# Two stages of a six-stage decoder share one block of programs: the routed experts' closing norm and the first input products of a state space layer

## The chip, the core and the metric

The kernel runs on one core of a Trainium2 chip, in one launch. The metric is the device time of that core in microseconds. In the order in which this text names them, the engines are TensorE (PE, matrix products and transposes), VectorE (DVE), ScalarE (ACT), GpSimd (POOL) and SyncE (SP, which issues most transfers). Each runs its own program in order and meets the others only through semaphores.

## The reference

Six stages run over 2048 tokens of width 256, in fp32. Each ends with the sum with its input and a norm over the 256 features. Stages 3 and 4 are those that the change touches.

```python
x = _layernorm(x + _L0_attn_ref(x, ...))              # stage 1: attention
x = _layernorm(x + _L0_xattn_ref(x, ctx, ctx, gamma)) # stage 2
x = _layernorm(x + _L0_ffn_ref(x, ...))               # stage 3: top 2 of 8 experts + a shared one
x = _layernorm(x + _L1_attn_ref(x, ...))              # stage 4: state space layer
x = _layernorm(x + _L1_xattn_ref(x, ctx, mask, ...))  # stage 5
x = _layernorm(x + _L1_ffn_ref(x, ...))               # stage 6: experts with LoRA

# stage 4, with u = x
zxbcdt = u @ W_in.T
z, xBC, dt = jnp.split(zxbcdt, [D_INNER, D_INNER + CONV_DIM], axis=-1)
for k in range(D_CONV):                               # 4 taps along the tokens
    conv = conv + xp[:, k:k + l, :] * conv_w[:, k]
xBC = silu(conv)
dt = softplus(dt + dt_bias)
y = _chunked_scan(xh, dt, -exp(A_log), Bh, Ch, D)     # decays exp(segsum(dt*A))
y = group_norm(y * silu(z)) * norm_weight
return y @ W_out.T
```

## The kernel before

The 2048 tokens are 16 tiles of 128 tokens (on the 128 partitions), and 4 chunks of 4 tiles. `resid` holds the tokens between stages as tiles, `residT` the same values turned, with the features on the partitions, as the next stage's products need them. One Python function for each stage opens one `nc.Block` with a hand written program for each of the five engines; the order inside an engine is the order of the code. The block's end is an event of every engine, in which POOL also drains its queue, and before each new function `recycle` (L86 to L95) has a barrier over all engines, a clearing of all semaphores on POOL, and a second barrier. Nothing of one block therefore overlaps the next.

**Stage 3** (`layer0_experts`, L1196, block L1267, names with `c_`) first routes, then runs 39 slots of 128 gathered token rows through the expert weights (SP loads slot s's rows into `c_xrow`, in 4 buffers; POOL sends each slot's output away with an indirect transfer), then adds up by halves of a chunk: SP brings the rows back, DVE combines them and takes mean and variance (`combine`, L1400 to L1413), POOL makes scale and shift by `variance_power` (L1305 to L1311, the last of it `c_shift`). Behind that come tile by tile: ACT's `apply` (L1337, writes `resid`), PE's `turn_back` (L1575, two transposes into a bank `cps_x`), ACT's `turned_out` (L1342, copies the bank to `residT`, one tile behind `apply`). In this text that part, 609 to 630 us, is the turning stretch.

**Stage 4** (`layer1_state_space`, L1620, block L1705, names with `d_`) starts with the time steps: eight products of `d_wdt` (L2082), four transposes (L2087), then DVE's softplus chain of 17 steps (`d_x` L1950 to `d_dt` L1973). The input product is dealt as jobs; in PE's program a job is a `fill` of a bank `dps_ip` (L2011; two products of 128 x 512, or for `mixed` four transposes, L2017), on ACT `evacuate` (for a job that is convolved, L1804 into `d_pad` and L1805 into `d_acc`; L1798 for the gate z), on DVE `convolve` (L1888, three instructions a job), on ACT `activate` (L1813). `own` are the eleven jobs of chunk 0 in their order: 0 to 5 the six that are convolved, 6, 7 and the next two of the gate, `mixed` at place 8. The scan goes by tiles q: PE's `segments` (L2030), ACT's `decay` (L1819), PE's `products` (L2042), DVE's `time` and `weigh`. After `products(0)` a loop over 23 slots runs to the stage's end at 827 us.

The constants of stage 4 are loaded at the head of SP's program: `d_wdt`, `d_bias`, `d_alog` for the time steps, `d_win` (768 KB) with two small ones for the convolution, then `d_wz` and the rest with `d_wout`.

Of the kernel before, what the change touches and what calls it, by code (L numbers as in the profile page):

```python
# [25 lines left out]
P = 128  # L26
# [35 lines left out]
class Kernel:  # L62
# [26 lines left out]

    def recycle(self):  # L90
# [1092 lines left out]
def experts_weights(k, ctx):  # L1183

    k.ahead, k.ahead_in = [], k.sem("c_weights_in")
    w = {}
    for name, shape, dt in (("wr", [P, KD, 32], F32), ("descending", [P, NE], F32), ("tables", [P, 256], F32),
                            ("lower", [P, P], BF16), ("wsg", [P, KD, SHARED], F32), ("wsu", [P, KD, SHARED], F32),
                            ("wsd", [P, 3, D], F32), ("wgu", [P, KD, NE, 2 * EF], F32), ("wd2", [EF // 2, NE, 2, D], F32)):
# [3 lines left out]
    return w  # L1193


def layer0_experts(k, w):  # L1196

# [9 lines left out]
    routed = nc.dram_tensor("routed", (2 * NTOK + XSLOTS * P, D), F32, kind="Internal").ap()  # L1207
    with ExitStack() as ctx:
# [10 lines left out]

        lg, best, cand = sb("lg", [P, TILES, E]), sb("best", [P, TILES, E]), sb("cand", [P, TILES, E])  # L1220
        masks, maxima = many(2, "mask", [P, TILES, E]), many(2, "max", [P, TILES])
        top, ex, total = sb("top", [P, TILES]), sb("ex", [P, TILES, E]), sb("total", [P, TILES])
        gate = many(2, "gate", [P, TILES])
# [4 lines left out]
        xr = sb("xr", [P, TILES, ROW])  # L1228
        acc = sb("acc", [P, TILES, D])
# [4 lines left out]
        back = [many(2, f"back{n}", [P, TPC, D]) for n in range(2)]  # L1234
# [7 lines left out]
        ltT = sb("ltT", [P, CHUNK])  # L1242
# [20 lines left out]

        def live(s):
            return 0 <= s < XSLOTS

        with nc.Block() as block:  # L1267
            @block.sync
            def _(sp):
                for n in range(2):  # L1270
                    sp.wait_ge(scattered[n], 16 * TILES)
                for s in range(XSLOTS):
                    if s >= 4:
                        sp.wait_ge(x_turned, s - 3)
                        sp.wait_ge(target_done, s - 3)
                    sp.dma_start(xrow[s % 4][:], k.xrows[s * P:(s + 1) * P, :]).then_inc(x_in[s % 4], 16)
                for v in range(4):
                    sp.wait_ge(sent[v], 16 * len(range(v, XSLOTS, 4)))
                for h in range(2 * NCHUNK):
                    c, half = divmod(h, 2)  # L1280
                    if h >= 2:
                        sp.wait_ge(back_in[h % 2], 32 * (h // 2))
                    if h >= 4:
                        sp.wait_ge(r_done, 2 * (h - 3))
                    for n in range(2):
                        first = n * NTOK + h * 2 * P
                        sp.dma_start(back[n][c % 2][:, 2 * half:2 * half + 2, :], routed[first:first + 2 * P, :].rearrange("(t p) f -> p t f", p=P)
                                     ).then_inc(back_in[h % 2], 16)

            @block.gpsimd  # L1290
            def _(gp):
                def scatter(t, n):
                    gp.indirect_dma_start(k.xrows[:], bass.IndirectOffsetOnAxis(ap=place_int[n][:, t:t + 1], axis=0),  # L1293
                                          xr[:, t, :], None).then_inc(scattered[n], 16)

                def send(s):
                    gp.wait_ge(out_done, s + 1)
                    gp.wait_ge(target_done, s + 1)
                    gp.indirect_dma_start(routed[:], bass.IndirectOffsetOnAxis(ap=target[s % 8][:], axis=0),  # L1299
                                          out[s % 4][:], None).then_inc(sent[s % 4], 16)  # L1300

                def variance_power(c):
                    u = c % 2
                    gp.wait_ge(mv_done, TPC * (c + 1))
                    gp.tensor_scalar(rstd[u][:], mv[u][:, :, 1], EPS, None, ALU.add).then_inc(eps_done, 1)  # L1305
                    gp.wait_ge(eps_done, c + 1)
                    gp.tensor_tensor(rstd[u][:], rstd[u][:], k.mhalf[:, 0:TPC], ALU.pow).then_inc(rstd_done, 1)
                    gp.wait_ge(rstd_done, c + 1)
                    gp.tensor_tensor(shift[u][:], mv[u][:, :, 0], rstd[u][:], ALU.mult).then_inc(product_done, 1)
                    gp.wait_ge(product_done, c + 1)  # L1310
                    gp.tensor_scalar(shift[u][:], shift[u][:], -1.0, None, ALU.mult).then_inc(shift_done, 1)  # L1311

                gp.wait_ge(placed, 2)
                gp.wait_ge(rows_copied, TILES + 2)
# [303 lines left out]


def layer1_state_space(k):  # L1620

# [1445 lines left out]
```

## Time and profile before

| | us |
|---|---|
| median of 3 runs | 1281.39 |
| the runs | 1274.37, 1281.39, 1285.85 |
| profiled execution, its own time | 1271.11 |
| span of the profile | 1269.0 |
| stage 3, closing part (shared expert, combine, turning stretch) | 592 to 630 |
| last work of stage 3 to first product of stage 4 | 630.3 to 637.8 |
| stage 4 | 637.8 to 827.8 |

The time lies 2.1 us over the span, which is what comes before the first and after the last recorded instruction. The profiled execution is 10.3 us shorter than the median and inside the range of the runs. TensorE's clock has two levels, and a granted clock of 1.00 or 0.50 means the upper or the lower, and a figure between a mixture within the stretch.

### The profile page before, as it was taken

What the parts mean: (1) busy time and instruction counts of PE and PEld (TensorE: products, weight loads), DVE (VectorE), ACT (ScalarE), POOL (GpSimd) and SP (SyncE); (2) the same over time, 40 slices, a digit from 0 to 9 for tenths busy, and PEclk for the clock granted to TensorE, in tenths of its full rate; (3) what the DMA queues carried; (4) which work ended last, traced back from release to release, by engine and by line L of the source; (5) the groups of instructions that cost most, each with busy time, mean ns of one, the idle gap of its engine ahead of it and who ended that gap; (6) DMA issues with size and microseconds to landing.
All of it is one profiled execution on the core that took longest, in us unless ns stands there. A gap on an engine that the chain in (4) does not pass through costs nothing. (4 is left out here: it accounts for less than half of the span.)

```text
span 1269.0 us, 20972 instructions
## 1 busy us (share of the span) xinstructions
PE 1112.9 (88%) x7484; PEld 662.5 (52%) x7484; DVE 781.2 (62%) x1531; ACT 575.9 (45%) x1199; POOL 455.1 (36%) x692
## 2 busy tenths in 40 slices
PE   6888779988888588999579998789998899999997
PEld 3566544454443245776234455567786343545455
DVE  4889887888884322333667677736566355555554
ACT  2666516766677301333455664256664322122120
POOL 6999852545542263333224445421111000000001
PEclk7999969999999799999789999989999899999999
DMA  6658244655652023333323000000000000000000
GB/s 217 202 174 275 81 124 122 150 137 148 146 130 53 25 84 96 105 109 101 99 65 141 1 1 1 1 1 2 2 2 1 25 1 0 9 9 9 8 9 25
DMA packets 73115, 91.72 MB, mean 72 GB/s; under 512 B 12691, under 2 KB 61997, under 8 KB 72333
## 3 DMA queue, kind: packets, MB, share of 16 engines
q1 hardware_dynamic: 68595, 80.72, 22.6%
q0 software_dynamic: 3408, 9.34, 2.1%
q8 instruction: 62, 1.02, 0.4%
q10 hardware_dynamic: 1010, 0.31, 0.1%
q14 instruction: 40, 0.33, 0.1%
HBM read 55.37 MB, written 29.17 MB: 67 GB/s over the span
## 5 line engine op out<-in xcount | busy, mean ns | idle before, releaser
L919 ACT ACTIVATE a_late<-a_qkv 128x512 f32<-128x512 f32 x128 | 77.2, 603 | 58.9 <-PE a_qkv L996 58.9
L2546 POOL TENSOR_SCALAR f_rstd<-f_mv 128x1 f32<-128x1 f32 x16 | 3.8, 240 | 267.9 <-DVE f_mv L2685 267.8
L867 DVE TENSOR_REDUCE b_nm<-a_s 128x4 f32<-128x1024 f32 x64 | 78.0, 1219 | 29.9 <-PE a_s L965 29.8
L2630 DVE TENSOR_TENSOR f_prod<-f_sg,f_kept 128x512 f32<-128x512 f32 (+1 forms) x48 | 33.2, 692 | 97.9 <-ACT f_kept L2575 95.0
L2755 PE MATMUL fps_h<-residT,w_f_w 128*128 128x512 f32 x176 | 83.9, 617 | 2.4 <-DVE f_inner L2667 2.4
L867 DVE TENSOR_REDUCE b_nm<-a_pt 128x4 f32<-128x1024 f32 x64 | 76.7, 1198 | 1.5 <-PE a_pt L965 1.5
L919 ACT ACTIVATE a_late<-a_y 128x512 f32<-128x512 f32 x128 | 76.9, 600 | 0.0
L2569 ACT ACTIVATE f_sg<-fps_h 128x512 f32<-128x512 f32 (+1 forms) x24 | 14.3, 596 | 126.6 <-PE fps_h L2774 109.8
L1011 PE MATMUL a_o<-a_late,b_vt 128*32 128x256 f32 x1024 | 69.2, 389 | 0.0
L1299 POOL DMA_INDIRECT routed<-c_out,c_target x39 | 37.5, 962 | 67.4 <-ACT c_out L1371 67.1
L1888 DVE SCALAR_TENSOR_TENSOR d_acc<-d_pad,d_cw,d_acc 128x512 f32<-128x512 f32 x72 | 57.8, 810 | 1.7
L351 POOL TENSOR_TENSOR a_nrm<-a_ss,phalf 128x20 f32<-128x20 f32 x16 | 57.0, 3560 | 4.2 <-DVE a_ss L473 4.2
L2755 PEld LDWEIGHTS fps_h<-residT,w_f_w 128*128 128x128 f32 x176 | 33.8, 196 | 42.9 <-issue 38.5
L1547 PE MATMUL cps_h<-c_wgu,c_xT 128*128 x156 | 52.7, 461 | 0.7 <-ACT c_xT L1359 0.6
L1486 DVE TENSOR_TENSOR c_hid<-c_sg,cps_h 128x176 f32<-128x176 f32 x39 | 13.2, 338 | 63.2 <-issue 50.6
L839 POOL TENSOR_TENSOR a_rest<-a_rest 128x256 f32<-128x256 f32 x16 | 11.6, 725 | 96.8 <-DVE a_rest L892 96.8
L1737 POOL TENSOR_TENSOR d_rs<-d_ms,mhalf 128x4 f32<-128x4 f32 x16 | 22.4, 1401 | 65.6 <-DVE d_ms L1945 65.6
L2011 PE MATMUL dps_ip<-residT,d_win 128*128 128x512 f32 x96 | 44.6, 598 | 0.3 <-ACT d_zs L1798 0.2
L1293 POOL DMA_INDIRECT xrows<-c_xr,c_place_int x32 | 31.1, 971 | 34.6 <-DVE c_xr L1456 19.3
L2569 ACT ACTIVATE f_sg<-f_kept 128x512 f32<-128x512 f32 (+1 forms) x24 | 15.1, 630 | 60.1 <-DVE f_kept L2635 60.1
L1566 PE MATMUL cps_o<-c_wd,c_hT 88*128 x156 | 40.1, 380 | 0.0
L1011 PEld LDWEIGHTS a_o<-a_late,b_vt 128*32 128x32 f32 x1024 | 26.9, 110 | 25.1 <-issue 14.0
(425 smaller groups left out, 2895.8 us busy)
## 6 DMA issues: line engine op xcount, KB each, us to landing
kparts<-a_rest SPq DMA_DIRECT2D x48, 192.0 KB, 3.2
a_rest<-a_rest SPq DMA_DIRECT2D x64, 128.0 KB, 3.1
xrows<-in_c_fill SPq DMA_DIRECT2D x13, 387.0 KB, 4.4
c_xrow<-xrows SPq DMA_DIRECT2D x39, 129.0 KB
c_back<-routed SPq DMA_DIRECT2D x16, 256.0 KB, 3.3
a_front<-kparts SPq DMA_DIRECT2D x12, 288.0 KB
a_front<-qparts SPq DMA_DIRECT2D x36, 96.0 KB
qparts<-b_xp SPq DMA_DIRECT2D x48, 64.0 KB, 2.8
```

The lines of the kernel that those rows point to most:

```text
L351: gp.tensor_tensor(nrm[v][:], ss[v][:], k.phalf[:, 0:H20], ALU.pow).then_inc(rooted, 1)
L867: dve.tensor_reduce(nm[s % 2][:, 4 * n:4 * n + 4].rearrange("p (g h) -> p g h", h=2), s1[step % 2][:], AX.X, ALU.max, negate=True).then_in ...
L919: act.activation(pr[g % 8][:], s2[g % 2][:], ACT.Exp, scale=SCALE).then_inc(s2_out, 1)
L1011: ins = pe.matmul(o_ps[32 * j:32 * j + 32, q % 2, :], vt[x % 2][:, lh, g, :], pr[g % 8][:, lh, :], start=(lh == 0), stop=(lh == KD - 1))
L1293: gp.indirect_dma_start(k.xrows[:], bass.IndirectOffsetOnAxis(ap=place_int[n][:, t:t + 1], axis=0), xr[:, t, :], None).then_inc(scattered[ ...
L1299: gp.indirect_dma_start(routed[:], bass.IndirectOffsetOnAxis(ap=target[s % 8][:], axis=0), out[s % 4][:], None).then_inc(sent[s % 4], 16)
L1547: ins = pe.matmul(h_ps[s % 2][:, 0:2 * F], xT[s % 2][:, kd, :], wgu[:, kd, ds(e, 1), :].rearrange("p a f -> p (a f)"), start=(kd == 0), st ...
L1566: ins = pe.matmul(o_ps[:, s % 2, 0:D], hT[s % 2][:, c, :], wd2[:, ds(e, 1), c, :].rearrange("p a f -> p (a f)"), start=(c == 0), stop=(c = ...
L1888: ins = dve.scalar_tensor_tensor(out=acc[v][:], in0=pad[v][:, :, tap:tap + T], scalar=cw[:, m, tap:tap + 1], in1=acc[v][:], op0=ALU.mult, ...
L2011: ins = pe.matmul(bank[:], win[:, kd, m * P:(m + 1) * P] if m < XT else wz[:, kd, (m - XT) * P:(m - XT + 1) * P], k.residT[:, kd, c * CHUN ...
L2630: dve.tensor_tensor(prod[n % 2][at], sg[n % 2][at], up, ALU.mult).then_inc(prod_done, 1)
L2755: pe.matmul(h_ps[j][:], (w1, w3)[j][:, kd, m * P:(m + 1) * P], k.residT[:, kd, c * CHUNK:(c + 1) * CHUNK], start=(kd == 0), stop=False)
```

## The change

The five programs of stage 3 become plain functions `sync`, `gpsimd`, `scalar`, `vector`, `tensor` that stage 4's block calls at the head of its own programs. Four of them take a hook `between` that stage 4 fills. The barrier pair and the clearing between all stages are gone (`recycle` is empty); the semaphores of the stages before are cleared on POOL at the start of stage 3 and at the start of stage 5 (`release`), without a barrier of their own beside the block's. Stage 4 takes over stage 3's PSUM banks: `cps_h` for `dps_ip`, `cps_t` for `dps_out`, `cps_o` for `dps_y`, `cps_x` for `dps_seg` and `dps_g`. The diff, cut to its core and without changes of indentation:

```diff
     def recycle(self):
-        self.nc.all_engine_barrier()
-        self.nc.clear_and_free_semaphores(self.sems)
-        self.nc.all_engine_barrier()
-        self.sems = []
+        pass
...
     # stage 3, SyncE, inside its loop over slots
             sp.dma_start(xrow[s % 4][:], k.xrows[s * P:(s + 1) * P, :]).then_inc(x_in[s % 4], 16)
+            between(sp, s)
...
     # stage 3, ScalarE
-    for t in range(TILES):
-        apply(t)
-        if t >= 1:
-            turned_out(t - 1)
-    turned_out(TILES - 1)
+    between(act, -1)
+    for c in range(NCHUNK):
+        for t in range(TPC * c, TPC * (c + 1)):
+            apply(t)
+            if t > TPC * c:
+                turned_out(t - 1)
+        turned_out(TPC * c + TPC - 1)
+        between(act, c)
...
     # stage 4, SyncE
+    def between(sp, s):
+        if s == 12:
+            for dst, src in dt_consts:
+                sp.dma_start(dst[:], io[src]).then_inc(dt_const, 16)
+        elif s == 14:
+            for dst, src in conv_consts:
+                sp.dma_start(dst[:], src).then_inc(conv_const, 16)
+        elif s == 16:
+            sp.dma_start(wz[:], io["d_win"][:, :, XT * P:]).then_inc(gate_const, 16)
+        elif s in (18, 20, 22):
+            for dst, src in consts[s - 18:s - 16]:
+                sp.dma_start(dst[:], io[src]).then_inc(const, 16)
+    experts.sync(sp, between)
...
     # stage 4, ScalarE
+    def between(act, c):
+        if c == -1:
+            act.wait_ge(dt_const, 16 * len(dt_consts))
+            act.activation(an[:], alog[:], ACT.Exp).then_inc(an_exp, 1)
+        elif c == 0:
+            act.wait_ge(const, 16 * len(consts))
+            for g in range(G):
+                ins = act.activation(wout[:, g, :], wout[:, g, :], ACT.Copy, scale=nw[:, g:g + 1])
+            ins.then_inc(wout_done, 1)
+            act.wait_ge(conv_const, 16 * len(conv_consts))
+            act.wait_ge(padded, 4)
+        elif c == 1:
+            evacuate(own[0])
+        elif c == 2:
+            evacuate(own[1])
+            evacuate(own[2])
+        else:
+            evacuate(own[3])
+    experts.scalar(act, between)
     act.activation(ltT[:], lt_ps[:], ACT.Copy).then_inc(lt_out, 1)
     act.activation(e[:], ab[:], ACT.Exp, scale=-1.0).then_inc(e_done, 1)
-    for n in own[:4]:
-        evacuate(n)
-    decay(0)
     activate(("in", 0, 0))
     evacuate(own[4])
     activate(("in", 0, 1))
     evacuate(own[5])
     activate(("in", 0, 2))
     evacuate(own[6])
-    evacuate(own[7])
     activate(("in", 0, 3))
+    evacuate(own[7])
+    decay(0)
     evacuate(own[8])
...
-    for g in range(G):
-        ins = act.activation(wout[:, g, :], wout[:, g, :], ACT.Copy, scale=nw[:, g:g + 1])
...
     # stage 4, VectorE
+    experts.vector(dve)
+    for n in own[:4]:
+        convolve(n)
...
-    for n in slot_jobs[-1]:
-        if jobs[n][1] == 0:
+    for n in own[4:]:
             convolve(n)
...
     # stage 4, TensorE
+    def between(pe, c):
+        pe.wait_ge(left.rT_out, TPC * (c + 1))
+        for n in (own[0:1], own[1:3], own[3:4], [])[c]:
+            fill(n)
+    experts.tensor(pe, between)
...
-    for n in own[:4]:
+    for n in own[4:8]:
         fill(n)
     segments(0)
-    for n in slot_jobs[-1][4:]:
+    for n in slot_jobs[-1][8:]:
         fill(n)
     products(0)
```

POOL's `between` sets the padding of `d_pad` after chunk 0's `variance_power`. The experts' weights also change places in memory and in the order of their loads in stage 1 (the largest, `c_wgu`, first).

TensorE, from the shared expert's last product to the first segment sums. Before:

```order
L1528 MATMUL cps_o<-c_wsd,c_hid_s 128x256 x12
L1575 MATMUL cps_x<-ident,resid 128x128 x32
L1267 UNCONDITIONAL_BRANCH
L1998 UNCONDITIONAL_BRANCH
L2082 MATMUL dps_out<-residT,d_wdt 32x512 x8
L2087 MATMUL dps_out<-ident,d_dtm 128x128 x4
L2011 MATMUL dps_ip<-residT,d_win 128x512 x8
L2030 MATMUL dps_seg<-d_dam,d_later 128x512
L2011 MATMUL dps_ip<-residT,d_win 128x512 x4
L2011 MATMUL dps_ip<-residT,d_wz 128x512 x4
L2017 MATMUL dps_ip<-ident,d_xc 128x128 x4
L2011 MATMUL dps_ip<-residT,d_wz 128x512 x4
```

And with the change:

```order
L1580 MATMUL cps_x<-ident,resid 128x128 x8
L2049 MATMUL cps_h<-residT,d_win 128x512 x2
L1580 MATMUL cps_x<-ident,resid 128x128 x8
L2049 MATMUL cps_h<-residT,d_win 128x512 x4
L1580 MATMUL cps_x<-ident,resid 128x128 x8
L2049 MATMUL cps_h<-residT,d_win 128x512 x2
L1580 MATMUL cps_x<-ident,resid 128x128 x8
L2128 MATMUL cps_t<-residT,d_wdt 32x512 x8
L2133 MATMUL cps_t<-ident,d_dtm 128x128 x4
L2049 MATMUL cps_h<-residT,d_win 128x512 x4
L2049 MATMUL cps_h<-residT,d_wz 128x512 x4
L2068 MATMUL cps_x<-d_dam,d_later 128x512
```

Four fills (8 products) stand between the turns of the chunks, in cps_h, four more ahead of the segment sums, and the two branches of the block's change are gone.

VectorE, from the last mean and variance of stage 3 on. Before:

```order
L1410 BN_STATS c_stats<-c_acc 128x6 x2
L1413 BN_AGGR c_mv<-c_stats 128x2 x2
L1267 UNCONDITIONAL_BRANCH
L1877 UNCONDITIONAL_BRANCH
L1950 TENSOR_TENSOR d_x<-dps_out,d_bias 128x128
L1953 TENSOR_SCALAR d_q<-d_x 128x128
L1955 TENSOR_TENSOR d_ab<-d_x,d_q 128x128
```

With the change:

```order
L1416 BN_STATS c_stats<-c_acc 128x6 x2
L1419 BN_AGGR c_mv<-c_stats 128x2 x2
L1923 SCALAR_TENSOR_TENSOR d_acc<-d_pad,d_cw,d_acc 128x512 x12
L1990 TENSOR_TENSOR d_x<-cps_t,d_bias 128x128
L1993 TENSOR_SCALAR d_q<-d_x 128x128
L1995 TENSOR_TENSOR d_ab<-d_x,d_q 128x128
L1997 TENSOR_SCALAR d_s<-d_e 128x128
```

Twelve of the eighteen convolution instructions, which stood behind the softplus chain, now stand ahead of it.

ScalarE, from the fourth evacuation of chunk 0 on. Before:

```order
L1804 ACTIVATE d_pad<-dps_ip 128x8x64
L1805 ACTIVATE d_acc<-dps_ip,d_cb,d_cw 128x512
L1819 ACTIVATE d_es<-dps_seg 128x512
L1813 ACT_TABLE_LOAD
L1813 ACTIVATE d_xc<-d_acc 128x512
L1804 ACTIVATE d_pad<-dps_ip 128x8x64
L1805 ACTIVATE d_acc<-dps_ip,d_cb,d_cw 128x512
L1813 ACTIVATE d_bT<-d_acc 128x512
L1804 ACTIVATE d_pad<-dps_ip 128x8x64
L1805 ACTIVATE d_acc<-dps_ip,d_cb,d_cw 128x512
L1813 ACTIVATE d_cT<-d_acc 128x512
L1798 ACTIVATE d_zs<-dps_ip 128x512 x2
```

With the change:

```order
L1828 ACTIVATE d_pad<-cps_h 128x8x64
L1829 ACTIVATE d_acc<-cps_h,d_cb,d_cw 128x512
L1878 ACTIVATE d_dtm<-cps_t 128x512
L1880 ACTIVATE d_e<-d_ab 128x128
L1837 ACT_TABLE_LOAD
L1837 ACTIVATE d_xc<-d_acc 128x512
L1828 ACTIVATE d_pad<-cps_h 128x8x64
L1829 ACTIVATE d_acc<-cps_h,d_cb,d_cw 128x512
L1837 ACTIVATE d_bT<-d_acc 128x512
L1828 ACTIVATE d_pad<-cps_h 128x8x64
L1829 ACTIVATE d_acc<-cps_h,d_cb,d_cw 128x512
L1837 ACTIVATE d_cT<-d_acc 128x512
```

The first decay (its `d_es`) moves behind the evacuations and activations of own 4 to 7, and gets a table load of its own ahead of it and one behind.

## Rows read from the trace of the kernel before

**Rows 1.** The page's head: the span, and TensorE's busy time.
```profile
span 1269.0 us, 20972 instructions
...
PE 1112.9 (88%) x7484; PEld 662.5 (52%) x7484; DVE 781.2 (62%) x1531; ACT 575.9 (45%) x1199; POOL 455.1 (36%) x692
```

**Rows 2.** Busy time of each engine by stretch, mean granted clock.
```profile
core 0: us, PE busy (x) PEld busy (x) DVE busy (x) ACT busy (x) POOL busy (x), PEclk, DMA share, GB/s
611.00:631.00 20.00, 9.68 (x33) 4.10 (x32) 13.03 (x40) 12.83 (x32) 5.73 (x12) 0.65 0.19 57
622.00:630.00 8.00, 5.50 (x16) 2.31 (x16) 2.03 (x7) 6.27 (x17) 1.70 (x4) 0.50 0.00 0
634.00:671.00 37.00, 29.05 (x82) 11.51 (x83) 23.97 (x37) 21.12 (x36) 13.42 (x16) 0.91 0.18 56
671.00:827.00 156.00, 138.34 (x756) 80.07 (x754) 110.90 (x212) 77.19 (x129) 71.01 (x104) 0.99 0.08 29
```

**Rows 3.** Timeline (start, us busy; in brackets the idle before): end of the experts.
```profile
623.73 0.30 DVE L1413 BATCH_NORM_AGGREGATE c_mv<-c_stats 128x2 f32<-128x6 f32 x2
...
626.10 0.60 ACT L1337 ACTIVATE resid<-c_acc,c_shift,c_rstd 128x256 f32<-128x256 f32 x1 [1.28 <-POOL c_shift L1311]
```

**Rows 4.** Timeline of 629 to 645 us: the end of one block, the next one's start.
```profile
629.89 0.38 ACT L1342 ACTIVATE residT<-cps_x 128x256 f32<-128x256 f32 x1 [0.38 <-PE cps_x L1575]
...
633.97 0.28 POOL L1753 MEMSET d_pad<- 128x24 f32 x4 [7.90 <-POOLq L95]
...
637.75 3.51 PE L2082 MATMUL dps_out<-residT,d_wdt 128*32 128x512 f32 x16 [7.90 <-DMA d_alog<-in_d_alog]
...
642.76 0.29 DVE L1950 TENSOR_TENSOR d_x<-dps_out,d_bias 128x128 f32<-128x128 f32 x1 [18.73 <-PE dps_out L2087]
...
644.49 0.60 ACT L1804 ACTIVATE d_pad<-dps_ip 128x512 f32<-128x512 f32 x1 [0.51 <-PE dps_ip L2011]
...
644.98 0.77 ACT L1805 ACTIVATE d_acc<-dps_ip,d_cb,d_cw 128x512 f32<-128x512 f32 x1
```

**Rows 5.** Timeline of 645 to 690 us: the state space layer's start.
```profile
649.52 16.35 DVE L1888 SCALAR_TENSOR_TENSOR d_acc<-d_pad,d_cw,d_acc 128x512 f32<-128x512 f32 x18
...
652.17 1.10 PE L2030 MATMUL dps_seg<-d_dam,d_later 128*128 128x512 f32 x2 [2.66 <-POOL d_dam L1724]
...
653.92 1.28 ACT L1813 ACT_TABLE_LOAD   x1
...
655.22 0.63 ACT L1813 ACTIVATE d_xc<-d_acc 128x512 f32<-128x512 f32 x1
...
660.97 0.60 PE L2017 MATMUL dps_ip<-ident,d_xc 128*128 128x128 f32 x4
...
668.88 0.65 PE L2042 MATMUL dps_g<-d_cT,d_bT 128*64 128x256 f32 x4
...
670.15 1.70 ACT L1860 ACTIVATE d_wout<-d_wout,d_nw 128x256 f32<-128x256 f32 x4
```

**Rows 6.** Instructions of L1267, the experts' block: duration in ns, start.
```profile
L1267 POOLq DRAIN  x1: 6177/6177/6177, 625.8 to 625.8; - x1
```

**Rows 7.** The same of L1705, the state space layer's block.
```profile
L1705 POOLq DRAIN  x1: 339/339/339, 825.0 to 825.0; - x1
```

**Rows 8.** Timeline behind that block's end.
```profile
828.08 0.42 ACT L2220 ACTIVATE e_junk<-resid 128x256 f32<-128x256 f32 x1 [0.29 <-PEq L1705]
```

**Rows 9.** Timeline, four 512-column products at the lower clock.
```profile
446.48 3.61 PE L1516 MATMUL cps_h<-residT,c_wsg 128*96 128x512 f32 x4 [4.54 <-DVE c_hid_s L1388]
```

**Rows 10.** Timeline, the same four at the upper clock.
```profile
593.80 1.88 PE L1516 MATMUL cps_h<-residT,c_wsg 128*128 128x512 f32 x4
```

**Rows 11.** DMA issues of 630 to 645 us: KB, us to landing.
```profile
d_win<-in_d_win SPq DMA_DIRECT2D x1, 768.0 KB, 4.6
...
d_wout<-in_d_wout SPq DMA_DIRECT2D x1, 512.0 KB, 3.8
```

**Rows 12.** The expert rows' loads, 500 to 592 us: ns of issue, first and last start.
```profile
L1276 SPq DMA_DIRECT2D c_xrow<-xrows x33: 319/320/327, 500.3 to 579.4; - x33
```

More of the change, by code:

```diff
@@ new lines, in sync @@
+        def sync(sp, between):
+            for n in range(2):
+                sp.wait_ge(scattered[n], 16 * TILES)
+            for s in range(XSLOTS):
+                if s >= 4:
+                    sp.wait_ge(x_turned, s - 3)
+                    sp.wait_ge(target_done, s - 3)
+                sp.dma_start(xrow[s % 4][:], k.xrows[s * P:(s + 1) * P, :]).then_inc(x_in[s % 4], 16)
+                between(sp, s)
+            for v in range(4):
+                sp.wait_ge(sent[v], 16 * len(range(v, XSLOTS, 4)))
+            for h in range(2 * NCHUNK):
+                c, half = divmod(h, 2)
+                if h >= 2:
+                    sp.wait_ge(back_in[h % 2], 32 * (h // 2))
+                if h >= 4:
+                    sp.wait_ge(r_done, 2 * (h - 3))
+                for n in range(2):
+                    first = n * NTOK + h * 2 * P
+                    sp.dma_start(back[n][c % 2][:, 2 * half:2 * half + 2, :], routed[first:first + 2 * P, :].rearrange("(t p) f -> p t f", p=P)
+                                 ).then_inc(back_in[h % 2], 16)
@@ L1617, in _ @@
+            for c in range(EARLY, NCHUNK):
+                for m in range(MS):
+                    shared_up(c, m)
+                shared_down(c)
+            for c in range(NCHUNK):
+                for t in range(TPC * c, TPC * (c + 1)):
                     turn_back(t)
+                between(pe, c)
+    k.second = Programs(sync, gpsimd, scalar, vector, tensor), Left(h_ps, o_ps, t_ps, x_ps, sdown, rT_out)
 def layer1_state_space(k):
@@ L1632, in layer1_state_space @@
     SLOTS = TILES + 7
+    experts, left = k.second
     jobs, slot_jobs = [], {}
@@ L1750, in variance_power, with between @@
                     gp.tensor_scalar(shift[v][:], shift[v][:], -1.0, None, ALU.mult).then_inc(shift_done, 1)
-                for n in range(4):
-                    gp.memset(pad[n][:, :, 0:CW - 1], 0.0).then_inc(padded, 1)
+                def between(gp, c):
+                    if c == 0:
+                        gp.wait_ge(left.sdown, NCHUNK)
+                        for n in range(4):
+                            gp.memset(pad[n][:, :, 0:CW - 1], 0.0).then_inc(padded, 1)
+                experts.gpsimd(gp, between)
                 gp.wait_ge(an_exp, 1)
@@ L1829, in apply @@
                     act.activation(k.resid[:, q, :], r[q % 4][:], ACT.Identity, bias=shift[q % 4][:], scale=rstd[q % 4][:]).then_inc(rn_done, 1)
[L1831 to L1832 removed]
+                own = [n for n in slot_jobs[-1] if jobs[n][1] == 0]
+                def between(act, c):
[14 more added lines that the diff above has]
+                        evacuate(own[2])
+                    else:
+                        evacuate(own[3])
+                experts.scalar(act, between)
                 act.wait_ge(lt_full, 1)
@@ L1945, in mean_square @@
                     dve.tensor_scalar(ms[q % 2][:], ss_ps, 1.0 / P, EPS, ALU.mult, ALU.add).then_inc(ms_out, 1)
+                experts.vector(dve)
+                own = [n for n in slot_jobs[-1] if jobs[n] in nth and jobs[n][1] == 0]
+                dve.wait_ge(conv_const, 16 * len(conv_consts))
+                for n in own[:4]:
+                    convolve(n)
                 st = Steps(dve, pre, 0)
@@ L2077, in put_out @@
                     ins.then_inc(p_full, 1)
+                own = [n for n in slot_jobs[-1] if jobs[n][1] == 0]
+                def between(pe, c):
[3 more added lines that the diff above has]
+                experts.tensor(pe, between)
                 pe.wait_ge(dt_const, 16 * len(dt_consts))
@@ L2088, in _ @@
                 ins.then_inc(dt_full, 1)
-                own = [n for n in slot_jobs[-1] if jobs[n][1] == 0]
-                for n in own[:4]:
+                for n in own[4:8]:
                     fill(n)
```

675 lines of the change are left out of this document (318 added, 357 removed).

## The prediction

> **What bounds the kernel now.** I read the page first. TensorE is busy for 1112.9 of 1269.0 us [rows 1], so time is saved where it stands still, and only there. The busy times by stretch show where that is near the change: in the turning stretch (611 to 631 us) it works 9.68 of 20 us at a mean clock of 0.65, at the start of stage 4 (634 to 671) 29.05 of 37, and in stage 4's loop 138.34 of 156 [rows 2]. What follows 671 runs in unchanged order, so a gain must be made ahead of `products(0)` and is then carried to the end.
>
> The timeline gives the chain through this place. DVE ends its last mean and variance at 624.03 and has nothing more to do for 18.73 us; ACT starts the last chunk's norm at 626.10, after 1.28 us idle behind POOL [rows 3]. The last copy to `residT` ends at 630.27, and PE's first product of stage 4 starts at 637.75, named as waiting for `d_alog`; POOL, which needs no data, is let go by the barrier (L95) at 633.97 [rows 4]. These 7.48 us hold no work. Then PE makes the time steps, DVE's chain starts at 642.76 [rows 4], all 18 convolution instructions follow it from 649.52 for 16.35 us, `segments(0)` is at 652.17, `mixed` at 660.97 and `products(0)` at 668.88 [rows 5].
>
> **Block's end, barriers, constants.** All 7.48 us go: the constants are asked for in the expert loop, some 60 us earlier, and the order is the only wait left. The time step products can then start when the last `residT` is out.
>
> **ACT in the turning stretch.** Ahead of chunk 3's first `apply` it now has two evacuations, each 0.60 + 0.77 = 1.37 us [rows 4], 2.74 together; 1.28 of it falls into the idle time of [rows 3]. So chunk 3 is 1.46 late and `residT` ready at 631.7 in place of 630.27. The scaling of `wout` (1.70 us, [rows 5]) now stands between chunk 0 and chunk 1; POOL's pace leaves ACT idle time there as well, and I cost it at nothing, at most 1.7. The table load for `d_an` comes ahead of the first `apply`, while ACT waits for chunk 0: nothing.
>
> **PE in the turning stretch.** Four fills are 8 products, two lots of four: 1.88 us a lot at the upper clock, 3.61 at the lower [rows 9, 10], and in 622 to 630 the clock is 0.50 with PE busy for 5.50 of 8 us [rows 2]. Turns of the next chunk queue behind them. Since a chunk's turns wait for ACT's `apply`, and PE idles for 10.3 us of 20, I put the fills in that idle time.
>
> **Time steps.** PE starts at 631.7, 6.0 us earlier than 637.75, DVE's chain at 642.76 - 6.0 = 636.7 if DVE is free. It now does 12 convolution instructions first, at 16.35 / 18 = 0.91 us, 10.9 in all from 624.03, to 634.9; the last three need the evacuation of own 3, which ends 1.37 behind the last `residT`, at 633.1, and so end at 635.8. Hidden by 0.9 us; were it not, each us is one lost. `segments(0)` comes at 652.17 - 6.0 = 646.1, and the other six convolution instructions, 5.45 us, start at 649.6 - 6.0 = 643.6 and end at 649.0 in place of 665.9.
>
> **From `segments(0)` to `products(0)`.** Before, four fills and waits for their banks lie between `segments(0)` and `mixed`: 660.97 - 652.17 = 8.8 us. These fills now run ahead of `segments(0)`, in the softplus chain's time, where PE waits anyhow. Behind `segments(0)` stays its own 1.10 / 2 and a handing over, say 0.9, then the part from `mixed` to `products(0)` as before, 668.88 - 660.97 = 7.91. That gives 646.1 + 0.9 + 7.9 = 654.9. DVE is no bar: its convolutions used to end 3.0 us ahead of `products(0)`, and 649.0 + 3.0 is 652.0. Two more table loads (1.28 each, [rows 5]) are in ACT's row; ACT waits at that place for PE or DVE between most jobs, so I take 0.5 of 2.6: `products(0)` at 655.4, 13.5 us earlier.
>
> The Trainium skill ("ScalarE: Activation LUTs", section "What ACT_TABLE_LOAD costs") gives a switch 1283 ns and a drain of some 1380 ns on top. Here the load takes 1.28 us and the activation behind it starts 1.30 after the load's start, at 655.22 [rows 5], so the trace shows the first part and not the second. By the page the two loads would be 5.3 us rather than 2.6, and the forecast 1274 if all the rest is exposed.
>
> **The drain.** At the end of stage 3's block POOL drains for 6.18 us, from 625.8 to 632.0 [rows 6], although its last computation is the one that ACT's `apply` at 626.10 waited for [rows 3]; at the end of stage 4's it takes 0.34 [rows 7]. What differs is that only stage 3 sends transfers from POOL (its indirect ones, 71). Joined, the one block end comes at 825.0, with these transfers in it. Bounds: 0 more, if the 6 us are a matter of how recent the transfers are, and 825.0 + 6.18 = 831.2 in place of the 827.9 at which stage 5's first work is let go (828.08, [rows 8]), 3.3 us, if they go with the transfers issued. I take 3.3: the sends ended well before 625.8, their data having been read back before the combines, so recency speaks weakly. The two clearings on POOL are hidden by work of stage 5 that doesn't need POOL at once.
>
> **The sum.** -13.5 + 3.3 = -10.2 us. 1271.11 of the profiled execution become 1260.9, and the median 1281.39 becomes **1271** us. The three runs of before spread by 0.9%, and 1% (12.8 us) is about what can be told from no change.
>
> **Rivals.** (A) The forecast, 1271, chance 0.45. (B) The drain is not paid again: -13.5, 1268, 0.17. For it speaks the 0.34 of [rows 7], against it that only block ends with such transfers behind them could tell.
>
> (C) TensorE's clock. It was at 0.50 in 622 to 630 and averages 0.91 in 634 to 671 [rows 2]. The fills may raise it sooner, or stay in a longer low stretch. If it is low through the softplus chain to behind `segments(0)`, eight products beyond `mixed` cost 2 x 1.73 = 3.5 more [rows 9, 10], and three fills between the chunks, 0.87 each longer, come into the turns' way, 2.6: +6, 1277, chance 0.22. If it stays at the upper level throughout, the time step products take half of 3.51 [rows 4] and the gain is 1.7 more; that lies in A's range.
>
> (D) Nothing comes of it: the later stages' waits take back the gain, since the whole of 671 to 827 is shared by PE (89%) and DVE (71%) [rows 2]. An earlier start moves all engines alike, so this needs a wait on something that does not move, which I don't find: 1281, chance 0.10.
>
> (E) The slower side: the constants' transfers hold up the expert rows. SP's queue gets 768 KB in the midst of a loop that loads a slot's rows every (579.4 - 500.3) / 32 = 2.47 us [rows 12], three slots ahead, 7.4 us. `d_win` alone takes 4.6 and `d_wout` 3.8 [rows 11], `d_wz` with its size between some 3.1 by the same rate, the small ones 3 together: 14.5 us of transfers in ten slots, 25 us. It decides when one row comes more than 7.4 us late. If the slots lose all 14.5, the net is +4.3: 1286, chance 0.06. At the outside each of the seven groups that share the queue costs a row's whole lead, and it is over 1294. Against it: the queue would have to be the one resource, and the three large loads are issued two slots, 4.9 us, apart.
>
> **How the numbers follow.** Likeliest A. The range is 1262 to 1279: it reaches under B by the run's own spread, and over C by the 1.7 of `wout`, and leaves out D's half and E. Faster by over 1% means under 1268.6: most of B, the upper clock, and the half percent of spread below A, 0.30. Slower by over 1% means over 1294, the outer part of E with whatever I have not seen: 0.05. Within 1%: 0.65.
>
> **What would show it.** In the profile after, the first product of `d_wdt` starts within 1 us of the last `residT`; that comes at 631 to 633; `d_x` within 5 us of it; `products(0)` at 654 to 657; a POOL drain of about 6 us at the shared block's end and stage 5's first work 3 us late against the loop's end. A DVE row that still convolves when the time steps are ready, an ACT that evacuates while turns wait, or fills that take 0.9 us each behind `segments(0)` would each show a step wrong. Rows of `c_xrow` that someone waits for would show E.

## The result

Before, the median of 18 runs is 1277.82 us (1273.70 to 1286.44), with the change 1267.34 (1261.85 to 1275.55). The ratio is 0.9923 with a 95% interval of 0.9905 to 0.9942: 9.8 us faster, between 7.4 and 12.1. That is under the 1% named in the prediction, and clear of zero. The first page lines of the changed kernel:

```profile
span 1266.5 us, 20948 instructions
...
PE 1118.9 (88%) x7484; PEld 668.5 (53%) x7484; DVE 779.9 (62%) x1531; ACT 577.8 (46%) x1201; POOL 455.7 (36%) x692
```

These spans, 1269.0 and 1266.5, are no measure of the change: single executions differ by more than it is worth. So every trace below is read from one fixed point, the end of stage 3's last mean and variance on DVE, called M (624.03 before, 628.92 after), the last thing in the chain that the order of work between the stages doesn't touch. M itself is 4.9 us later in the changed kernel's profile. Of this 1.5 us were there when stage 3 began (its first work on ACT is at 431.75 before, at 433.25 after), 2.4 arose ahead of the expert loop and 1.0 in it. No run shows it as a cost of the change: from that first work to M it is 192.3 us before and 195.7 here, but 193.0 when the same kernel is run again (e5, below), and 191.1 to 194.2 in all ten further profiles, which have the same constants loaded in the same places. Timeline of the changed kernel, in the order of the chain:

```profile
619.05 3.48 PE L2049 MATMUL cps_h<-residT,d_win 128*128 128x512 f32 x4 [0.47 <-ACT residT L1346]
...
625.58 5.40 PE L2049 MATMUL cps_h<-residT,d_win 128*128 128x512 f32 x8 [0.47 <-ACT residT L1346]
...
628.62 0.30 DVE L1419 BATCH_NORM_AGGREGATE c_mv<-c_stats 128x2 f32<-128x6 f32 x2
...
630.82 0.60 PE L1580 MATMUL cps_x<-ident,resid 128*128 128x128 f32 x4
...
631.23 0.38 ACT L1346 ACTIVATE residT<-cps_x 128x256 f32<-128x256 f32 x1 [3.57 <-PE cps_x L1580]
...
631.62 0.24 POOL L1315 TENSOR_SCALAR c_shift<-c_shift 128x4 f32<-128x4 f32 x1
...
635.96 1.11 ACT L1341 ACTIVATE resid<-c_acc,c_shift,c_rstd 128x256 f32<-128x256 f32 x2
...
639.45 0.38 ACT L1346 ACTIVATE residT<-cps_x 128x256 f32<-128x256 f32 x1 [0.25 <-PE cps_x L1580]
...
639.89 1.92 PE L2128 MATMUL cps_t<-residT,d_wdt 128*32 128x512 f32 x16 [0.47 <-ACT residT L1346]
...
643.29 0.29 DVE L1990 TENSOR_TENSOR d_x<-cps_t,d_bias 128x128 f32<-128x128 f32 x1
...
651.99 1.10 PE L2068 MATMUL cps_x<-d_dam,d_later 128*128 128x512 f32 x2 [0.27 <-POOL d_dam L1743]
...
652.93 0.60 PE L2055 MATMUL cps_h<-ident,d_xc 128*128 128x128 f32 x4
...
661.58 0.65 PE L2080 MATMUL cps_x<-d_cT,d_bT 128*64 128x256 f32 x4
```

The first time step product now starts 0.06 us behind the end of the last `residT` (639.83), where [rows 4] had 7.48 us. `mixed` follows `segments(0)` by 0.94 us, where [rows 5] had 8.8. But the last `residT` itself comes 10.9 us behind M, where it came 6.2. The middle rows show why: the two fills behind chunk 1's turns hold PE from 625.58 to 631, chunk 2's turns start at 630.82, ACT waits 3.57 us for them, then makes two evacuations, and chunk 3's `apply`, whose `c_shift` is ready at 631.86, starts at 635.96. Busy times of these stretches and of the loop of stage 4 (columns as in [rows 2]):

```profile
616.90:620.90 4.00, 2.74 (x8) 1.32 (x8) 4.00 (x12) 3.75 (x10) 2.06 (x4) 0.81 0.66 225
620.90:624.90 4.00, 2.94 (x10) 1.29 (x9) 4.00 (x15) 2.58 (x7) 0.77 (x2) 0.76 0.00 0
624.90:630.00 5.10, 4.63 (x9) 1.86 (x8) 5.06 (x16) 2.52 (x5) 2.11 (x5) 0.67 0.00 0
630.00:636.00 6.00, 3.21 (x13) 1.54 (x12) 2.10 (x4) 4.51 (x11) 2.90 (x5) 1.00 0.00 1
...
661.60:823.50 161.90, 143.78 (x763) 83.26 (x762) 111.52 (x213) 78.28 (x129) 71.59 (x104) 0.97 0.08 28
```

The clock is 0.67 to 1.00 between 616.9 and 636, where [rows 2] had 0.50 in 622 to 630. At the joint block's end stands what [rows 6] showed at stage 3's end. ACT's row is the first of stage 5, its last copy of stage 4 having ended at 823.55:

```profile
L1717 POOLq DRAIN  x1: 6168/6168/6168, 820.8 to 820.8; - x1
```

```profile
827.20 0.42 ACT L2267 ACTIVATE e_junk<-resid 128x256 f32<-128x256 f32 x1 [3.66 <-PEq L1717]
```

The difference of the two spans, 2.5 us, is made up so: M 4.9 later, `products(0)` 12.2 earlier against it, the loop of stage 4 3.1 longer (of which more at e5), the block's end 3.4 longer, and stages 5 and 6 1.6 shorter.

Two things in the parts ahead of the prediction are wrong. `recycle` isn't called before each stage: it is called once, between stages 3 and 4, and that one barrier pair is what the change removes. No number rests on that. And the titles of [rows 9, 10] speak of four products: in the timeline each 128 x 512 product of these kernels stands as two rows (the eight products of `d_wdt` are `x16` in [rows 4]), so the `x4` of [rows 9, 10] is two products, which is one fill. The orders count products, and their "four fills (8 products)" is right. The prediction's step on PE rests on the titles, and below it is told what it cost.

### The profile page after: what moved, and what is told of

It is laid out like the page before. It is cut to its first block and busy times, and to the rows that moved or that the text cites. A ratio compares the mean times of both kernels' runs of the same rounds, so it can differ in the third digit from the quotient of the medians.

```text
span 1266.5 us, 20948 instructions
## 1 busy us (share of the span) xinstructions
PE 1118.9 (88%) x7484; PEld 668.5 (53%) x7484; DVE 779.9 (62%) x1531; ACT 577.8 (46%) x1201; POOL 455.7 (36%) x692
## 5 line engine op out<-in xcount | busy, mean ns | idle before, releaser
L2049 PE MATMUL cps_h<-residT,d_win 128*128 128x512 f32 x96 | 48.5, 639 | 4.0 <-ACT d_acc L1829 1.7
```

The lines of the kernel that those rows point to most:

```text
L2049: ins = pe.matmul(bank[:], win[:, kd, m * P:(m + 1) * P] if m < XT else wz[:, kd, (m - XT) * P:(m - XT + 1) * P], k.residT[:, kd, c * CHUN ...
```

## The experiments

Positions in us behind M, each from one profiled execution (a row's start, or for `residT` its end, less the end of the last `c_mv` row), and the timed ratios to before. The same kernel run twice (the change and e5, e3 and e6) differs by 1.2 to 1.3 us in `products(0)`, but by 0.02 us at most in the way from `d_x` to it, so that column is the steady one:

| | last residT | d_x | products(0) | products(0) less d_x | stage 5 less last residT of stage 4 | ratio (95%) |
|---|---|---|---|---|---|---|
| before | 6.24 | 18.73 | 44.85 | 26.12 | 0.29 | 1 |
| the change | 10.91 | 14.37 | 32.66 | 18.29 | 3.65 | 0.9923 (0.9905 to 0.9942) |
| e5, again | 10.55 | 15.56 | 33.85 | 18.29 | 3.66 | 0.9926 (0.9894 to 0.9958) |
| e1 | 6.26 | 11.92 | 37.32 | 25.40 | 3.66 | 0.9981 (0.9958 to 1.0003) |
| e2 | 10.44 | 13.90 | 39.47 | 25.57 | 3.66 | 0.9999 (0.9980 to 1.0019) |
| e8 | 6.25 | 11.46 | 38.68 | 27.22 | 3.66 | 0.9968 (0.9933 to 1.0003) |
| e4 | 7.84 | 14.86 | 37.61 | 22.75 | 3.66 | 0.9965 (0.9942 to 0.9988) |
| e3 | 9.51 | 14.51 | 32.81 | 18.30 | 0.28 | 0.9923 (0.9899 to 0.9947) |
| e6, as e3 | 10.81 | 15.86 | 34.14 | 18.28 | 0.28 | 0.9895 (0.9857 to 0.9933) |
| e7 | 7.83 | 12.93 | 30.50 | 17.57 | 0.28 | 0.9879 (0.9843 to 0.9915) |
| e10 | 11.88 | 15.34 | 32.38 | 17.04 | 0.28 | 0.9894 (0.9859 to 0.9928) |
| e9 | 7.00 | 12.02 | 34.04 | 22.02 | 0.28 | 0.9885 (0.9845 to 0.9925) |

**e1, the join alone.** The hooks of ACT and PE are empty and the order behind the time steps is that of before.

```diff
-    for n in (own[0:1], own[1:3], own[3:4], [])[c]:
-        fill(n)
...
-    for n in own[4:8]:
+    for n in own[:4]:
         fill(n)
     segments(0)
-    for n in slot_jobs[-1][8:]:
+    for n in slot_jobs[-1][4:]:
         fill(n)
```

> The change with its joint block, early constants and banks, but the work in the order of before: nothing between the turns, the 11 jobs of chunk 0 filled and evacuated behind the time step products, all 18 convolution instructions behind the softplus chain, the first decay and the scaling of wout where they were. Theory 1 (the join gives the 7.5 us of empty time, the moved drain takes 3.7 back, the new order gives the rest): first product of d_wdt within 1 us of the last residT, products(0) some 7.5 us earlier than before against the last mean and variance of stage 3, stage 5's first work 4 us earlier; ratio to before 0.996 to 0.998. Rival (the join gives all, the new order nothing because the fills stand in the turns' way): 0.992, as fast as the change.

The timeline of e1:

```profile
628.88 0.38 ACT L1346 ACTIVATE residT<-cps_x 128x256 f32<-128x256 f32 x1 [0.38 <-PE cps_x L1580]
...
629.31 3.64 PE L2118 MATMUL cps_t<-residT,d_wdt 128*32 128x512 f32 x16 [0.47 <-ACT residT L1346]
...
660.32 0.65 PE L2072 MATMUL cps_x<-d_cT,d_bT 128*64 128x256 f32 x4
```

The busy times of e1 over the same stretch as in [rows 2]:

```profile
622.00:630.00 8.00, 4.79 (x18) 1.93 (x20) 1.00 (x5) 5.67 (x14) 2.92 (x6) 0.50 0.00 1
```

`products(0)` is at 37.32 behind M in place of 44.85: 7.53 us, the empty time. The last `residT` stays at 6.26. Behind it two small differences cancel. The time step products take 3.64 us at the lower clock, and `d_x` comes 5.66 us behind the last `residT`, where it was 5.01 with the empty time left out; from `d_x` to `products(0)` it is 25.40 us, where it was 26.12. The drain gives 3.4 back, so 4.2 are left; the timed 0.19% (2.4 us, up to 5.3) agrees. The join explains less than half of the gain, and the rival is out.

**e2 and e8, half of the new order each.** e2 is the change with fills 4 to 7 behind `segments(0)` again and ScalarE's order behind the time steps that of before, so `decay(0)` ahead of the first activation and own 9 and 10 evacuated ahead of the activation of job 5; e8 is e1 with the fills of own 0 to 7 ahead of `segments(0)` and `decay(0)` late, but nothing between the turns.

```diff
     # e2, TensorE
-    for n in own[4:8]:
-        fill(n)
     segments(0)
-    for n in slot_jobs[-1][8:]:
+    for n in slot_jobs[-1][4:]:
         fill(n)
...
     # e8, TensorE
-    for n in own[4:8]:
+    for n in own[:8]:
         fill(n)
...
     # e8, VectorE
-    for n in own[:4]:
-        convolve(n)
...
-    for n in own[4:]:
+    for n in own:
         convolve(n)
```

> The change, but the part behind the time steps in the order of before: fills 4 to 7 behind segments(0), decay(0) ahead of the first activation, no extra table loads. The fills and evacuations between the turns and the early convolutions stay. Theory 1 (the 8.8 us between segments(0) and mixed are gained by the fills ahead of it): products(0) comes 6 to 9 us later than in the change, ratio to before 0.998 to 1.000. Rival (DVE's early convolutions are what pulls products(0) forward, the place of fills 4 to 7 is free): same as the change, 0.992.

> e1 (joined, nothing between the turns, all 18 convolution instructions behind the softplus chain) with the other half of the new order: own 0 to 7 are filled ahead of segments(0), decay(0) behind the activation of job 3, with the two extra table loads. Theory (the two halves of the new order need each other: the convolutions bind here): mixed comes 5 us or more earlier than in e1, and products(0) stays within 1.5 us of e1's 37.3 us behind the last mean and variance; ratio 0.997 to 0.999. Rival (the fills ahead of segments(0) alone give the 7 us that e2 lacked against the change): products(0) at 30 to 33 us, ratio 0.991.

`segments(0)` of e2, VectorE's convolutions behind the softplus chain and the row of `products(0)`, in e2 (M at 624.82) and in e8 (M at 625.41):

```profile
646.65 2.05 PE L2068 MATMUL cps_x<-d_dam,d_later 128*128 128x512 f32 x2 [8.03 <-POOL d_dam L1743]
...
652.66 5.89 DVE L1923 SCALAR_TENSOR_TENSOR d_acc<-d_pad,d_cw,d_acc 128x512 f32<-128x512 f32 x6 [7.81 <-ACT d_acc L1829]
...
664.29 0.65 PE L2080 MATMUL cps_x<-d_cT,d_bT 128*64 128x256 f32 x4
```

```profile
642.91 16.35 DVE L1917 SCALAR_TENSOR_TENSOR d_acc<-d_pad,d_cw,d_acc 128x512 f32<-128x512 f32 x18
...
664.09 0.65 PE L2072 MATMUL cps_x<-d_cT,d_bT 128*64 128x256 f32 x4
```

Counted from `d_x`, so that the turning stretch drops out, the way to `products(0)` takes 25.4 us in e1, 25.6 in e2, 27.2 in e8 and 18.3 in the change. Neither half gains anything there; both together gain 7. With the fills early and the convolutions late DVE binds: in e8 it convolves without a pause until 659.26. With the convolutions early and the fills late PE and its banks do: in e2 PE stands for 8.03 us ahead of `segments(0)`, with fills 4 to 7 queued behind it, and DVE for 7.81 us until ACT has evacuated the first of them. Counted from M, with the turning stretch in it, e2 and e8 are 2.2 and 1.4 us later than e1, and the whole new order is 3.2 to 4.7 us earlier (32.66 to 34.14 against 37.32): the longer turning stretch takes back the rest of the 7. In e8 my expectation of `mixed` was wrong: it came 1 us earlier than in e1 and not 5, since eight fills ahead of `segments(0)` push that to 27.5 behind M (20.6 in e1) while they wait for their banks.

**e3 and e6, the drain paid early.** One line, run twice:

```diff
     for s in range(XSLOTS):
         send(s)
+    gp.drain()
     for c in range(NCHUNK):
         variance_power(c)
```

> The change with one drain of POOL put behind its last send, ahead of the first variance_power, where POOL waits 12 us for DVE. Theory (the 6.17 us of drain are owed once for the transfers that POOL issued, whenever it next drains): the drain at the shared block's end falls from 6.17 to about 0.34 us, stage 5's first work comes 3.7 us earlier, 823.5 by the clock of the change's profile; ratio to before 0.989. Rival (every drain behind such transfers takes 6 us, paid or not): the end keeps its 6.17 us, ratio 0.992 or, if the new one delays chunk 0's scale, up to 0.995.

> The same early drain as in e3, beside the change on one chip. Theory: stage 5's first work comes 0.3 us behind stage 4's last residT in place of 3.7; ratio to before 0.989, against 0.992 of e5. Rival (the 3.4 us are there in the trace but given back later, in stages 5 and 6): the trace as in the theory, the ratio that of e5.

The instructions of the new line and of the block's end in e3, then the first work of POOL behind it and the first of stage 5:

```profile
L1326 POOLq DRAIN  x1: 7500/7500/7500, 595.6 to 595.6; - x1
```

```profile
L1718 POOLq DRAIN  x1: 337/337/337, 814.1 to 814.1; - x1
```

```profile
609.39 0.42 POOL L1309 TENSOR_SCALAR c_rstd<-c_mv 128x4 f32<-128x4 f32 x1 [12.12 <-DVE c_mv L1420]
...
817.17 0.42 ACT L2268 ACTIVATE e_junk<-resid 128x256 f32<-128x256 f32 x1 [0.28 <-PEq L1718]
```

The 6.2 us are owed once, by the next drain after the transfers, be it 220 us after the last send (600.9 to 820.8 in the change): paid early, the drain runs from 595.6 to 603.1, 5.8 us of it behind POOL's last send (whose row ends at 597.27), and POOL's next work, which waits for DVE, is only at 609.39. And the end of the block falls to 0.34 us. In the trace it is worth 3.66 - 0.28 = 3.4 us in all five profiles with it, and it isn't given back later, as the rival of e6 had it: from stage 5's first work to the end of the span it is 443.0 us in e5 and in e6. In time, e3 missed the 0.989 that I expected: its ratio was that of the change, measured in another series of runs. Beside the change, on one chip, e6 gave 0.9895 against 0.9926, 4 us, with intervals of 4 to 5 us to either side. The times don't contradict 3.4 us, and don't prove it.

**e5, the change once more, and the length of the loop.**

> The change itself once more, so that the next three can be set beside it on one chip. Theory: ratio to before 0.992; last residT 9.5 to 11 us and products(0) 32.7 us behind stage 3's last mean and variance, as in the change's profile; the stretch from products(0) to stage 4's last residT is 158.8 us where the clock stays at 1.00 in it (as before, e2 and e3 show) and up to 6 us longer where it falls near its end. Rival (the longer loops of the change, e1 and e4 belong to their order of work): it is 162 us again, at a lower clock in the same place.

Stage 4's loop in e5, and in e6, whose loop is the same (columns as in [rows 2]):

```profile
663.00:822.00 159.00, 140.62 (x763) 81.10 (x762) 111.50 (x213) 78.28 (x129) 71.49 (x104) 0.99 0.08 29
```

```profile
663.50:828.50 165.00, 146.98 (x763) 84.15 (x762) 111.67 (x213) 78.23 (x129) 71.45 (x104) 0.95 0.08 28
```

From `products(0)` to stage 4's last `residT` it is 158.8 to 158.9 us before and in e2, e3, e5 and e8, but 162.0 in the change's first profile, 161.4 in e7, 163.6 to 163.8 in e4 and e10, and 165.0 to 165.2 in e1, e6 and e9. The same kernel stands on both sides (the change and e5, e3 and e6), with PE's busy time 6.4 us apart for the same 763 rows and everything else equal. So between these it is the granted clock of the one execution, and not the order; that the same holds for the other kernels, whose loop has the same work, is likely and not shown. It takes up to 6 us in a single profile, two thirds of what the change is worth, which is why only positions behind M are compared.

**e4 and e9, another spacing of the fills.** e4 puts one fill into each gap and own 3 behind the time step products:

```diff
-    for n in (own[0:1], own[1:3], own[3:4], [])[c]:
+    for n in own[c:c + 1] if c < 3 else []:
         fill(n)
...
     ins.then_inc(lt_full, 1)
+    fill(own[3])
     pe.wait_ge(lt_out, 1)
```

> The change with one fill (own 0, 1, 2) in each of the three gaps between the turns and own 3 behind the time step products, so that ACT has one evacuation ahead of chunk 3's first apply in place of two and PE two products less ahead of chunk 2's turns; own 2 and 3 are evacuated behind the ltT copy and convolved behind the softplus chain. Theory 2 (own 1 and 2 in one gap, at the lower clock, hold chunk 2's turns and then chunk 3's apply, some 4 to 5 us): last residT some 3 to 4 us earlier against the last mean and variance, and products(0) 1 to 3 us earlier, since two convolutions move behind the chain; ratio 0.990 to 0.991. Rival (DVE's two convolutions behind the chain cost what the turns gain): 0.992 or more.

e9 mends it: own 3 behind the transposes, own 2 evacuated ahead of the `ltT` copy, three jobs convolved ahead of the softplus chain; with the early drain and e7's order.

> e7 (early drain, gate evacuations ahead) with e4's spacing and its fault mended: one fill (own 0, 1, 2) in each gap, own 3 with 4 to 7 behind the time step transposes and not ahead of them, one evacuation ahead of chunk 3's apply, own 2 evacuated while PE makes the time step products, three jobs convolved ahead of the softplus chain in place of four. Theory (e4 lost by its fill ahead of the transposes and by six convolution instructions moved behind the chain): last residT 7.8 us behind the last mean and variance, d_x at 12 to 13, products(0) at 31.5 to 33, three moved instructions costing 2.7 of what the turns save; ratio 0.988 to 0.990, not to be told from e7. Rival (the turning stretch is what binds): products(0) at 28 to 30, ratio 0.986 or less.

The last `residT` and `products(0)` of e9 (M at 623.03):

```profile
629.65 0.38 ACT L1347 ACTIVATE residT<-cps_x 128x256 f32<-128x256 f32 x1 [0.25 <-PE cps_x L1581]
```

```profile
657.07 0.65 PE L2081 MATMUL cps_x<-d_cT,d_bT 128*64 128x256 f32 x4
```

In both the turning stretch is short, 7.8 and 7.0 us behind M, and `products(0)` is late all the same, 37.6 and 34.0: e4 was expected 1 to 3 us ahead of the change and came 5 behind it, e9 missed its 31.5 to 33 by 1. In e4 the fill of own 3 stands between the time step products and the transposes, the way from the last `residT` to `d_x` is 7.0 us (3.5 in the change, 5.0 in e5), and the way from `d_x` is 4.5 us longer than in the change, with two jobs more convolved behind the chain. In e9 it is 4.5 longer than in e7 with one such job, and ACT's rows behind `d_x` (635.05) tell why:

```profile
638.07 0.60 ACT L1829 ACTIVATE d_pad<-cps_h 128x512 f32<-128x512 f32 x1 [4.29 <-PE cps_h L2050]
638.56 0.77 ACT L1830 ACTIVATE d_acc<-cps_h,d_cb,d_cw 128x512 f32<-128x512 f32 x1
639.23 0.31 ACT L1881 ACTIVATE d_e<-d_ab 128x128 f32<-128x128 f32 x1
```

The exponential that the softplus chain needs stands behind the evacuation of own 3, whose fill I had moved behind the transposes: it starts 4.2 us behind `d_x`, in e7 0.9. That is 3.3 of the 4.5, a fault of mine in the order; by subtraction 1.2 are left for the moved job, which no run shows alone. So e9 doesn't tell whether the turning stretch binds; the rival's 28 to 30 was not reached. Its ratio is e7's within either interval, though its trace has `products(0)` 3.5 us later: the times can't resolve that.

**e7 and e10, the order behind `d_x`.** e7 has the early drain and the evacuations of own 9 and 10 ahead of the activation of job 5; e10 is e7 with `decay(0)` last.

```diff
     # e7, ScalarE
     activate(("in", 0, 4))
-    activate(("in", 0, 5))
     evacuate(own[9])
     evacuate(own[10])
+    activate(("in", 0, 5))
...
     # e10, besides
     evacuate(own[7])
-    decay(0)
     evacuate(own[8])
...
     activate(("in", 0, 5))
+    decay(0)
```

> e6 with ACT's evacuations of own 9 and 10 moved ahead of the activation of job 5, as they stood before the change. Theory (PE's last fills ahead of products(0) wait for these banks, 1.8 us in the change's trace, while ACT waits for DVE's last convolution): products(0) 31.3 to 32 us behind the last mean and variance, 0.7 to 1.3 us earlier than in e6; ratio not to be told from e6's. Rival (products(0) waits for the activation of job 5 itself): no earlier, or later by the evacuations' 1.07 us.

> e7 with decay(0) behind the activation of job 5, so that the chain from the last residT to products(0) has one switch of tables, as before the change, and not three. Theory (the two extra loads lie in ACT's waits, my term for them was 0.5 us): products(0) 0 to 0.8 us earlier against d_x than e7's 17.57 us, and the first weighing no earlier, since the decay now comes last; ratio that of e7. Rival (ACT is the bound there, the loads cost their full 2.56 us): products(0) 2 us or more earlier against d_x.

`d_x` and `products(0)` in e7, then in e10:

```profile
640.01 0.29 DVE L1991 TENSOR_TENSOR d_x<-cps_t,d_bias 128x128 f32<-128x128 f32 x1 [1.58 <-PE cps_t L2134]
```

```profile
657.58 0.65 PE L2081 MATMUL cps_x<-d_cT,d_bT 128*64 128x256 f32 x4
```

```profile
640.69 0.29 DVE L1991 TENSOR_TENSOR d_x<-cps_t,d_bias 128x128 f32<-128x128 f32 x1
...
657.73 0.65 PE L2081 MATMUL cps_x<-d_cT,d_bT 128*64 128x256 f32 x4
```

17.57 us from `d_x` in e7, 0.72 less than the change, at the low end of what was expected; 17.04 in e10, 0.53 less again. What follows comes earlier too: the first weighing is 0.4 us nearer to `d_x` than in e7, where I had expected no gain. So two fewer switches of tables, together with the place of the decay itself, are worth 0.5 us here, not 2.6. e7's turning stretch, the same code as e3's and e6's, took 7.8 us behind M where theirs took 9.5 and 10.8: with the clock at 1.00 in it throughout, in 612 to 635.

```profile
612.00:635.00 23.00, 16.03 (x63) 7.76 (x62) 22.04 (x56) 18.43 (x43) 9.88 (x21) 1.00 0.22 69
```

Of the versions tried e7 has the lowest ratio, 0.9879: 1.2% under before, though not told apart from e6, e9 and e10.

## Why the prediction was right, step by step

- **The time.** 1271 was predicted, 10.2 us under the median that was known; the measured gain is 9.8 (7.4 to 12.1). The median itself, 1267.3, is lower, because the longer series put before at 1277.8. In the traces the gain is 44.85 - 32.66 = 12.2 us at `products(0)`, less 3.4 at the drain: 8.8. Forecast A held, in its range; I had written -13.5 + 3.3. That it held so closely is in part luck: the turning stretch was put 3.2 us too short, and in this one profile a high clock behind it gave 1.5 back. In e5, the same kernel with a low clock there, the traces' gain is 44.85 - 33.85 - 3.4 = 7.6 us.
- **Block's end, barriers, constants: 7.48 us.** Measured alone in e1, 7.53. Right. Of the 7.48 the drain holds 1.7 (it ends at 632.0), the barriers and the clearing 2.0 (POOL works at 633.97), and the constants the last 3.8: PE's first row waits for `d_alog` [rows 4, 6].
- **The constants in the expert loop (rival E).** Nothing was held that can be told from noise. The rows' loads of the changed kernel, from 507 us on, where the 2.0 MB of constants are being moved too:

```profile
L1280 SPq DMA_DIRECT2D c_xrow<-xrows x32: 319/320/583, 507.1 to 584.3; - x32
```

  (584.3 - 507.1) / 31 is 2.49 us a slot, against 2.47 in [rows 12]. From the first of the 39 loads to the last it is 86.7 us before, 87.7 here, 86.3 in e1 and 88.3 in e5, all three with the constants among them.
- **The later stages (rival D).** They take nothing back: from stage 5's first work to the end of the span it is 440.9 us before and 439.3 with the change.
- **The turning stretch: the term that was mis-sized.** "Four fills are 8 products, two lots of four: 1.88 us a lot" took the row's `x4` for two fills; it is one. A fill costs 1.9 us at the upper clock and 3.5 at the lower (own 0: 3.48), so four take twice what I put into PE's idle time, and at the mixed clock of this profile the two behind chunk 1 take 5.40 us and keep ACT waiting for chunk 2's turns for 3.57. Rival C's prices for the lower clock were halved by the same count: with 1.73 us a fill, its 3.5 and 2.6 us would be 6.9 and 5.2. The last `residT` was put at 7.7 us behind M and came at 9.5 to 10.9, in e10 11.9, and only with the clock at 1.00 throughout (e7) at 7.8.
- **The clock (rival C).** It went neither the rival's way nor steadily the other. Without fills between the turns it is 0.50 there (e1, as [rows 2]). With them it moves between the levels, 0.67 to 1.00 in the stretches above, down to 0.57 over 4 us in e10 and at 1.00 throughout in e7. In the change, e2 and e10 it was high behind the turns too: the time step products take 1.92 us in place of 3.51, and from the last `residT` to `d_x` it is 3.5 us and not the 5.0 to 5.7 of before (its empty time left out) and e1, which gives back a part of the turning stretch's loss. In e3, e5, e6, e7 and e9 it was low just there, and the way is 5.0 to 5.1 us. Which it is belongs to the single execution: the change and e5 are one kernel.
- **The time steps.** `d_x` was put at 12.7 behind M and came at 14.4 (12.9 in e7). The twelve early convolutions were hidden as said, but with nothing to spare in this profile (0.9 us forecast): `d_x` starts at 643.29, 0.1 us behind its last transpose (642.53 + 0.66), as it did before, and DVE comes to it straight from the last of them. In e5, e3 and e7 DVE waited 1.5 to 1.6 us.
- **From `segments(0)` to `products(0)`.** 0.9 + 7.9 + 0.5 forecast, 9.59 measured (661.58 - 651.99). That the fills go into the chain's time was right, but the working named them alone. e2 and e8 show that their place is worth nothing without the early convolutions: the 8.8 us belong to both edits together.
- **Table loads.** 0.5 us taken, 0.53 measured (e10). The load took 1.28 us and the next activation started 1.29 after the load's start:

```profile
654.78 1.28 ACT L1837 ACT_TABLE_LOAD   x1
...
656.07 1.33 ACT L1837 ACTIVATE d_cT<-d_acc 128x512 f32<-128x512 f32 x2
```

  By the Trainium skill ("ScalarE: Activation LUTs", "What ACT_TABLE_LOAD costs") a drain of 1.38 us would follow; no row of this case shows it, and the measurement decides. The prediction's 1274 by that section of the Trainium skill added only the drains; an estimate with its whole 5.3 us in place of the 0.5 taken is 1276.
- **The drain.** 3.3 us taken, 3.36 measured (3.65 - 0.29), 6.168 us long as before. e3 settles what I chose on weak grounds: it goes with the transfers issued, not with how recent they are, and once paid it is gone. Rival B was wrong, and would have given 1268, a time that the runs can't tell from 1271.

What stays open is the time of the early drain (e3 and e6 differ by 0.3%), why the clock is high behind the turns in one execution and low in the next, and whether the loop's clock dips are as frequent in every order; single profiles can't say.

## What to carry to other kernels

When two blocks are joined, what the block's end did for free moves with it: look for drains and clearings that now fall on the last engine's path, and pay them in a stretch in which their engine waits anyway. Early work is worth only what the next bound lets through: here fills and convolutions moved ahead gave 0 each and 7 us together behind `d_x` (3 to 5 with the turning stretch they lengthen), so try both edits before dropping either. And count a row's `x` against the program's own order before pricing it.

## What the runs showed of the hardware

- POOL's drain behind its indirect transfers takes 6.2 us (5.8 behind the last send in e3), once, even 220 us after that send, and 0.34 us at the next block's end.
- TensorE's granted clock stood at 0.50, the lower level, all through the later turns while only the turns ran (before, e1). With four fills between them it moved between 0.57 and 1.00 from one execution to the next, and the time step products behind them took 1.92 us or up to 3.53.
- A load of ACT's tables takes 1.28 us, and the next activation starts 1.29 to 1.30 us after its start.
- One and the same loop took 158.8 or 165.0 us (PE busy 140.6 or 147.0) by the granted clock of the execution (e5, e6).
